# Attention's weighted values with the exps as stationary side of the product, and two banks for the score maxima

## What is computed

```python
x = x + _L0_xattn_ref(_layernorm(x, axis=-1), ctx_512, ctx_512)
x = x + _L0_ffn_ref(_layernorm(x, axis=-1), L0_ffn_router_w, L0_ffn_w1, L0_ffn_w2)

# of _L0_xattn_ref:
scores = jnp.einsum('bkgsd,bktd->bkgst', qh, kh) / scale
weights = jax.nn.softmax(scores, axis=-1)
out = jnp.einsum('bkgst,bktd->bkgsd', weights, vh)
```

## Time and profile before

| | us |
|---|---|
| median of 3 runs | 10124.08 (10117.09 to 10131.62) |
| the profiled execution, its own time | 10143.92 |
| its span | 10142.2 |
| from the start of the attention's first steps to the first step with expert work | 442 to 1418 |
| steps with attention and expert work | 1418 to 8443 |

### The profile page before, as it was taken

One profiled execution on the slowest core, in us unless ns is written; L12 is line 12 of the kernel. 1 busy time (PEld: TensorE's weight loads), 2 busy tenths in 40 slices (PEclk: granted clock), 3 DMA queues, 4 the chain that ended last, 5 costly groups with the idle time before them and its releaser, 6 DMA issues. The chain is left out here.

```text
span 10142.2 us, 169689 instructions
## 1 busy us (share of the span) xinstructions
PE 9157.7 (90%) x55016; PEld 4601.1 (45%) x55016; DVE 5165.7 (51%) x10907; ACT 3662.6 (36%) x5426; POOL 2411.2 (24%) x3894
## 2 busy tenths in 40 slices
PE   4466689999999999999999999999999999989989
PEld 3322234444444444444444444444444444444457
DVE  7766665555555555555555555555555554222212
ACT  3444444333333333443333433333443343200001
POOL 0022222222222222222222222222222222211111
PEclk8688889999999999999999999999999999999999
DMA  9742134444444444444444444444444444454444
GB/s 364 298 186 75 53 104 127 134 134 130 122 130 123 134 133 131 128 132 119 131 134 130 120 133 121 132 134 131 127 133 119 131 136 128 122 189 145 160 167 165
DMA packets 455196, 1431.29 MB, mean 141 GB/s; under 512 B 90088, under 2 KB 110568, under 8 KB 454128
## 3 DMA queue, kind: packets, MB, share of 16 engines
q1 hardware_dynamic: 360240, 1132.12, 33.2%
q0 software_dynamic: 94016, 287.65, 12.2%
HBM read 1034.41 MB, written 408.21 MB: 142 GB/s over the span
## 5 line engine op out<-in xcount | busy, mean ns | idle before, releaser
L866 PE MATMUL e_y<-e_xt,e_w 128*128 128x512 f16 x14520 | 3518.6, 380 | 0.0
L950 ACT ACTIVATE a_p<-a_sc,a_escale 128x512 f32<-128x512 f32 x2048 | 1406.3, 687 | 3621.2 <-PE a_sc L696 3555.8
L1342 DVE TENSOR_REDUCE a_nmax<-a_mx 128x2 f32<-128x512 f32 x2048 | 1411.6, 689 | 1897.6 <-PE a_mx L713 1882.6
L866 PEld LDWEIGHTS e_y<-e_xt,e_w 128*128 128x128 f16 x14520 | 1372.6, 98 | 1597.5 <-issue 244.4
L887 PE MATMUL e_y<-e_w,e_yt 128*128 128x512 f16 x7480 | 1857.7, 380 | 0.0
L713 PE MATMUL a_mx<-a_ks,a_qs 96*128 96x256 f16 x4096 | 816.9, 282 | 564.0 <-DVE a_nmax L1342 559.2
L682 PE MATMUL a_pv<-a_p,a_v 128*64 128x512 f32 x4096 | 1104.1, 664 | 0.0
L1156 POOL TENSOR_TENSOR a_xres<-a_att,a_xres 128x128 f32<-128x128 f32 x1024 | 469.3, 479 | 2424.9 <-DVE a_att L1367 1886.5
L887 PEld LDWEIGHTS e_y<-e_w,e_yt 128*128 128x128 f16 x7480 | 691.0, 98 | 767.6 <-issue 127.4
L713 PEld LDWEIGHTS a_mx<-a_ks,a_qs 96*128 96x128 f16 x4096 | 370.0, 99 | 1078.2 <-DVE a_nmax L1342 684.9
L696 PE MATMUL a_sc<-a_qs,a_ks 128*128 128x512 f16 x2048 | 794.8, 388 | 58.0 <-ACT a_p L950 45.7
(11 more groups left out here) (231 smaller groups left out, 9787.7 us busy)
## 6 DMA issues: line engine op xcount, KB each, us to landing
e_w<-w_parts SPq DMA_DIRECT2D x935, 512.0 KB, 3.6
f_w<-w_parts SPq DMA_DIRECT2D x153, 512.0 KB, 4.9
w_parts<-w_parts SPq DMA_DIRECT2D x136, 512.0 KB, 4.9
h_w<-w_parts SPq DMA_DIRECT2D x136, 512.0 KB, 6.0
a_x<-in_x SPq DMA_DIRECT2D x64, 1024.0 KB, 5.8
a_xres<-in_x SPq DMA_DIRECT2D x64, 1024.0 KB, 7.8
out<-a_xres SPq DMA_DIRECT2D x64, 1024.0 KB, 8.6
xn_parts<-a_xhl SPq DMA_DIRECT2D x64, 1024.0 KB, 9.6
```

The costliest lines, as they stand in the source:

```text
L866: last = pe.matmul(Y[:, bank, :], w1r[:, t % RING, h, pw, :], xT[:, px, h, :], start=r == 0, stop=r == 3 * HT - 1)
L950: act.activation(PT[:, kv % 2, h, tt, :], SC[:, :], ACT.Exp, scale=escale[:, sp_:sp_ + 1]).then_inc(n["exps"], 1)
L1342: dve.reduce_max(nmax[:, half, kv * G + 2 * gp:kv * G + 2 * gp + 2], MX[:, :, :], AX.X, negate=True).then_inc(n["maxed"], 1)
```

## The change

- `values` exchanges the sides. Stationary is now a 128 x 128 fp32 piece of `PT` (128 keys by 128 queries), moving are the 34 columns of `V1` (32 values and 2 of ones). For each half c of the queries and each query head g of the group there are two such products, one for each half tt of the keys: 16 fp32 matmuls for 4. The result has queries on the partitions and is written to `PV`, 34 of 64 columns for each c and g.
- `values_out`, `OS`, `turn_o` and `OT` are gone, with their semaphores. `o_out` reads `PV` itself, and `values` waits for the `o_out` of the group before (`o_done`) where it had waited for `values_out`. `attended` adds rows in plain order.
- `MX` gets the bank of `OT` and has two banks. `max_score` and `max_out` take them in turn (q % 2), and `max_score` waits for the maxima of two before, not of the one before.
- In PE's order `values` moves from behind `max_score` 1 to behind `max_score` 2 and `turn_max`.

```diff
-        V1 = sb("a_v", [P, 2, KV, 2 * D], F32)
+        V1 = sb("a_v", [P, 2, KV, D + 2], F32)
-        MX = ps("a_mx", [P, 2, S], F32)
+        MX = ps("a_mx", [P, 2, 2, S], F32)
-        PV = ps("a_pv", [P, 2 * S], F32)
-        OT = ps("a_ot", [P, 4, P], F32)
+        PV = ps("a_pv", [P, 2, G, 2 * D], F32)
@@ values
-                at_least(pe, n["o_there"], b * 8 + kv)
-                for tt in range(2):
-                    for h in range(2):
-                        last = pe.matmul(PV[2 * D * h:2 * D * (h + 1), :], V1[:, tt, kv, :],
-                                         PT[:, kv % 2, h, tt, :], start=tt == 0, stop=tt == 1)
+                at_least(pe, n["o_done"], b * 8 + kv)
+                for c in range(2):
+                    for g in range(G):
+                        cols = slice((g % 2) * S + c * P, (g % 2) * S + (c + 1) * P)
+                        for tt in range(2):
+                            last = pe.matmul(PV[:, c, g, 0:D + 2], PT[:, kv % 2, g // 2, tt, cols],
+                                             V1[:, tt, kv, :], start=tt == 0, stop=tt == 1)
@@ max_score
-                at_least(pe, n["maxed"], b * 32 + (4 * kv + q))
+                at_least(pe, n["maxed"], b * 32 + (4 * kv + q - 1))
...
-                    last = pe.matmul(MX[:, g2, :], QS[0:96, kv, g * S + half * P:g * S + half * P + P],
+                    last = pe.matmul(MX[:, q % 2, g2, :], QS[0:96, kv, g * S + half * P:g * S + half * P + P],
@@ turn_o: gone
-                for c in range(2):
-                    for g in range(2):
-                        last = pe.transpose(OT[:, 2 * c + g, :], OS[:, g * S + c * P:g * S + c * P + P],
-                                            ident[:, :])
@@ iteration, PE
                     max_score(i, k, par, 0)
-                    turn_o(i, k)
...
                     max_score(i, k, par, 1)
-                    values(i, k, par)
...
                     max_score(i, k, par, 2)
                     turn_max(i, k)
+                    values(i, k, par)
@@ ScalarE: values_out gone
-                    act.activation(OS[:, :], PV[:, :], ACT.Copy).then_inc(n["o_there"], 1)
@@ o_out
-                    dve.wait_ge(n["o_turned"], b * 8 + (u + 1))
+                    dve.wait_ge(n["pv"], b * 8 + (u + 1))
...
-                    dve.reciprocal(orec[:, u % 2, :, :], ot[:, :, :, D]).then_inc(n["o_recip"], 1)
+                    dve.reciprocal(orec[:, u % 2, :, :], PV[:, :, :, D]).then_inc(n["o_recip"], 1)
...
-                    dve.tensor_tensor(att[:, u % 2, :, :, :], ot[:, :, :, 0:D],
+                    dve.tensor_tensor(att[:, u % 2, :, :, :], PV[:, :, :, 0:D],
```

More of the change, by code:

```diff
@@ L390, in fuse @@
         KS = sb("a_ks", [P, 2, KV, S], F16)
-        V1 = sb("a_v", [P, 2, KV, 2 * D], F32)
+        V1 = sb("a_v", [P, 2, KV, D + 2], F32)
         PT = sb("a_p", [P, 2, 2, 2, 2 * S], F32)
-        OS = sb("a_o", [P, 2 * S], F32)
-        att = sb("a_att", [P, 2, 4, 2, D], F32)
+        att = sb("a_att", [P, 2, 2, G, D], F32)
         xres = sb("a_xres", [P, 2, 2, H], F32)
@@ L408, in fuse @@
         mhl = sb("a_mhl", [2 * G, 2, 2, S], F16)
-        orec = sb("a_orec", [P, 2, 4, 2], F32)
+        orec = sb("a_orec", [P, 2, 2, G], F32)
         logit = sb("a_logit", [P, 2, E], F32)
@@ L464, in fuse @@
                      "q_turned", "q_there", "k_turned", "k_there", "max_scores", "maxed",
-                     "max_turned", "max_high", "max_low", "scores", "exps", "pv", "o_there", "o_turned",
+                     "max_turned", "max_high", "max_low", "scores", "exps", "pv",
                      "o_recip", "o_done", "x1_done",
@@ L789, in turn_rows @@
                 last.then_inc(turned, 1)
[L791 to L796, removed]
-                for c in range(2):
-                    for g in range(2):
-                        last = pe.transpose(OT[:, 2 * c + g, :], OS[:, g * S + c * P:g * S + c * P + P],
-                                            ident[:, :])
-                last.then_inc(n["o_turned"], 1)
             def turn_max(i, k):
@@ L1089, in iteration @@
                     k_out(i, k, par)
-                    values_out(i, k)
                     experts(i, 8 * k + 5, par, fused)
@@ L1105, in _ @@
             pool.memset(ksrc[:, :, :, 3 * D + 2:P], 0.0).then_inc(filled, 1)
-            pool.memset(V1[:, :, :, D:2 * D], 1.0).then_inc(filled, 1)
+            pool.memset(V1[:, :, :, D:D + 2], 1.0).then_inc(filled, 1)
             def newton(sem_, b, y, w):
@@ L1154, in attended @@
                     for c in range(2):
-                        to = xres[:, bp, c, u * P:(u + 1) * P].rearrange("p (h g d) -> p g h d", h=2, g=2)
-                        pool.tensor_tensor(to, att[:, u % 2, 2 * c:2 * c + 2, :, :], to, ALU.add)\
+                        to = xres[:, bp, c, u * P:(u + 1) * P]
+                        pool.tensor_tensor(to, att[:, u % 2, c, :, :].rearrange("p g d -> p (g d)"), to, ALU.add)\
                             .then_inc(n["x1_done"], 1)
@@ L1341, in max_out @@
                         at_least(dve, n["max_turned"], b * 4 + (kv // 2) - 3)
-                    dve.reduce_max(nmax[:, half, kv * G + 2 * gp:kv * G + 2 * gp + 2], MX[:, :, :],
+                    dve.reduce_max(nmax[:, half, kv * G + 2 * gp:kv * G + 2 * gp + 2], MX[:, q % 2, :, :],
                                    AX.X, negate=True).then_inc(n["maxed"], 1)
@@ L1361, in o_out @@
                 if on(b):
-                    dve.wait_ge(n["o_turned"], b * 8 + (u + 1))
+                    dve.wait_ge(n["pv"], b * 8 + (u + 1))
                     at_least(dve, n["x1_done"], b * 16 + 2 * (u - 1))
-                    ot = OT[:, :, :].rearrange("p q (v d) -> p q v d", v=2)
-                    dve.reciprocal(orec[:, u % 2, :, :], ot[:, :, :, D]).then_inc(n["o_recip"], 1)
+                    dve.reciprocal(orec[:, u % 2, :, :], PV[:, :, :, D]).then_inc(n["o_recip"], 1)
                     dve.wait_ge(n["o_recip"], b * 8 + (u + 1))
-                    dve.tensor_tensor(att[:, u % 2, :, :, :], ot[:, :, :, 0:D],
-                                      orec[:, u % 2, :, :].unsqueeze(3).to_broadcast([P, 4, 2, D]),
+                    dve.tensor_tensor(att[:, u % 2, :, :, :], PV[:, :, :, 0:D],
+                                      orec[:, u % 2, :, :].unsqueeze(3).to_broadcast([P, 2, G, D]),
                                       ALU.mult).then_inc(n["o_done"], 1)
```

## The result

The changed kernel takes 10952.71 us in the median of 4 runs (10928.67 to 10980.17), the kernel before 10121.22: a ratio of 1.0821, 95% interval 1.0794 to 1.0848. The direction was forecast, the size was not: +831 us where +236 stood on record. The profiled execution took 10928.67 us.

The account below looks back on a forecast made before the run. PE's row of instructions was taken to bound the stretch with expert work; 10143.9 + 477 - 160 - 80 = 10381 us profiled, forecast 10360 as the profiled run lies 20 us over the median; 8-in-10 range 9500 to 10560.

Parts of the forecast that it names:

- The price of a pair: New values on PE: each 128-column fp32 load with its matmul costs 0.11 us, 32 a group, net +1.13 us, +477 us.
- The rival of 0.055 us: New values on PE: loads run at one column a cycle, net -0.63 us a group, 9530 us in all; chance 0.17.
- The second bank: Maxima with expert work: PE waits less for VectorE's reductions, -160 us, with ends 0 and -295.
- The steps of attention alone: Stretch from 442 to 1418 us: dearer groups against fewer waits, sum -80 us, from -200 to +126.
- the term 90 x 1.13/0.81: Steps of attention alone: 90 groups' net extra PE time at clock 0.81, +126 us, if loads slow with the clock.
- The terms +126 and -200: Steps of attention alone: +126 us of PE work for 90 groups, 200 of 261.6 us of maxima waits gone.
- The clock with expert work: PE during the new products: a clock fall to 0.50 would make each group dearer and upset the sum; no size given.
- the forecast's own step that moves the stall to the third maxima: Where the loop begins anew: PE meets VectorE's stall about 3.0 us of work later, saving 2.6 us each, 68 us.
- the two dearer rivals: Load and matmul not overlapping, 10850 us, chance 0.07; second bank giving nothing back, 10730 us, chance 0.05.
- the rival of load and matmul in series (10850): New values on PE: no overlap at 34 columns, 0.14 us a pair, net +2.1 us a group, 10850 us; chance 0.07.
- That the rest cost nothing: ScalarE, `o_out`, POOL, the order of `values` and the wait for `o_done` were taken as free; 13 us if uncovered.
- The slot that the prediction gives POOL: POOL's copy of the next values and the expert rows' gather start later but have a slot of 16.6 us.

Follow-up runs that it names:

- old_two_banks: Kernel before the change plus a second bank for the maxima, old values kept, turned result in the values' bank: 9921.76 us, ratio 0.9814.
- wide64: Changed kernel with 64 moving columns in place of 34 in the new products: 10780.19 us, ratio 1.0651 to the kernel before.
- wide128: Changed kernel with 128 moving columns in place of 34, and one bank for the maxima again: 10761.31 us, ratio 1.0645 to the kernel before.
- fill: Changed kernel, products singly after expert matmuls; in steps without expert work an idle 512-column matmul behind each product: 10189.31 us, ratio 1.0079 to the kernel before.
- mixed: Kernel before with two maxima banks; new products, one after each expert matmul, only in steps with expert work: 9875.72 us, ratio 0.9760.

## Why the forecast went the right way and fell short

- **The price of a pair** was the step in doubt, and it held: 0.11 us forecast, 0.109 measured, a group 3.49 us for 3.52, and 447 us in the stretch with expert work and some 15 in the last steps for 477. The row that decided was the right one, the old values' load of 64 columns at two cycles a column, and not the transposes' load. The rival of 0.055 us took the start's transposes to run at half clock, by the length of their loads; the trace's clock records begin only later, so that reading is not shown. The Trainium skill's rule ("TensorE: Matmul & The Clock Gate", section on loading the stationary operand: columns divided by 1.2, in ns) gives 107 ns for 128 columns, an estimate from that page; this trace agrees, with 109 from one pair to the next, though each load is recorded at 192.
- **The second bank** held: -162 us of waits with expert work for -160, and 159 us when it was added alone. The stall where the loop begins anew stayed, at up to 6.6 us.
- **The steps of attention alone** failed: -80 forecast, +285 measured. The failing step is the term 90 x 1.13/0.81. It took over the clock of 0.81 from the kernel before, though the change takes away the 1.87 us of 512-column matmuls in each group; with them, and two banks, old_two_banks runs these steps at 0.83. With 34 columns the clock is 0.52, and every instruction of these steps pays, not the group alone: +330 us, of which some 210 lie in the groups. Without the clock the steps would have gained 44 us, by the sum. (The terms +126 and -200 make -74, where the sum on record has -80.)
- **The clock with expert work** was no term of the sum at all: +199 us. It stood in the last paragraph as something that would upset the sum, without a price, a chance or a place among the rivals. Two things lie in it. Some 127 us are falls behind a group without a wait; no row of the kernel before showed one, since all its falls in that stretch came behind waits. The other 75 or so are groups at half clock right behind the stall, and the rows for that were there: the clock of 0.50 after it, and the forecast's own step that moves the stall to the third maxima, with `values` next. A rival "the clock falls with the new products" could have been priced as well: 644 busy us at 0.81 are 644 x 0.81/0.50 = 1043 us at half clock, an estimate of some 400 us for the first steps alone.
- The range, 9500 to 10560, ended at the forecast's own upper end, with the two dearer rivals left out; the measured time lies 393 us above it, and near the rival of load and matmul in series (10850), whose mechanism did not occur: that nearness is chance.
- That the rest cost nothing (the copy gone, `o_out` from another bank, the wait for `o_done`) held: PE's waits for `o_done` come to 1.2 us on the page's line for L682. The slot that the prediction gives POOL, 7025/422 = 16.6 us, is 17.2 with the 408 groups that the stretch holds; nothing hung on it.

## What to carry to other kernels

When an edit trades columns that stream past the array for loads of its stationary side, count the clock as a resource that the edit can spend: a row of matmuls that is bound by its loads can leave PE without a gap and still lower the clock for the work behind it. Look at what kept the clock up in the stretch where there is least other work, and put load-bound products between wide matmuls, where their first loads hide as well. Do not put a dear group right behind a known stall, where the clock is down. And ask of a change with two parts whether one needs the other: here the bank alone gave 1.9%.

## What the runs showed of the hardware that I had not expected

- The granted clock fell (0.51 in the row from 2992.50 to 2995.90) behind 3.5 us of PE work without a gap: 32 pairs of 128-column fp32 loads and 34 moving columns. In the stretch with expert work it did so behind 74 of 408 groups, and behind none in wide64 and wide128. With the same loads the first steps ran at a mean clock of 0.52 in the changed kernel, 0.54 in wide64, 0.79 in wide128 and 0.83 in fill.
- A fp32 load of 128 columns is recorded at 192 ns for a real product and at 140 for a transpose. At full clock the products' pairs are 0.109 us apart, as far as the start's transposes (0.110), whose clock is not on record.
- Two matmul instructions of one fp32 product cost 0.14 us behind a 512-column matmul and 0.218 in a row: the first load hides behind the matmul ahead, the second doesn't.
- The engine that stands where a loop's body begins anew can be another one after an edit: VectorE before, PE too in mixed, 98.5 us in 23 times.
